# Two runs of eight: a second wait in front of the ninth indirect transfer of a row scatter and of a row gather

## The reference

```python
    h = _L0_tok_ref(x, codebook, W1, b1, W2, b2)               # take rows, gelu(q W1 + b1) W2 + b2
    h = h + _L0_attn_ref(_layernorm(h), Wz, bz, Wh, bh)        # two minGRU layers
    h = h + _L0_ffn_ref(_layernorm(h), w1s, w2s, w3s, W1, W2, W3, Wg)

    # the feed-forward stage
    shared = geglu(xf, w1s, w2s, w3s)                          # (gelu(x w1) * (x w2)) w3
    idx = jnp.argmax(xf @ Wg, axis=-1)
    for e in range(8):
        final = final + jnp.where((idx == e)[:, None], geglu(xf, W1[e], W2[e], W3[e]), 0.0)
    return shared + final
```

## Time and profile before

| | |
|---|---|
| device time, median of 3 | 533.82 us (533.76 to 534.25) |
| profiled execution, its own time | 534.71 us |
| its span | 533.1 us |
| PE busy | 503.7 us, 94% |
| DVE, ACT, POOL busy | 323.8, 247.2, 74.5 us |
| mean granted clock of PE | 0.982 of full |
| scatter: 16 transfers issued | 247.44 to 268.38 us |
| gather of results: 16 transfers issued | 493.62 to 514.55 us |

### The profile page before, as it was taken

The page is one execution under the profiler, slowest core; times in us unless marked ns, Lnnn a source line. Parts: engine busy times, 40 slices in busy tenths (PEclk is TensorE's granted clock), DMA queues, the critical chain, the costliest instruction groups (busy, mean ns, idle before and its releaser), DMA issues.

```text
span 533.1 us, 9472 instructions
## 1 busy us (share of the span) xinstructions
PE 503.7 (94%) x2942; PEld 441.1 (83%) x2943; DVE 323.8 (61%) x533; ACT 247.2 (46%) x374; POOL 74.5 (14%) x97
## 2 busy tenths in 40 slices
PE   8999998998999997999899799999999999999975
PEld 7798887886887786888788689898898988888864
DVE  2547677787587777657443847734865568383325
ACT  2656673564663453334243645724563555362311
POOL 4422030000000000003710001000100001000740
PEclk9999998999999999999999899999999999999978
DMA  5941412000020002202332338440546165200324
GB/s 169 317 164 29 144 39 80 0 1 1 2 80 1 1 0 80 79 1 81 132 114 90 123 145 271 142 148 30 183 163 205 42 253 192 105 20 20 88 71 157
DMA packets 20586, 52.81 MB, mean 99 GB/s; under 512 B 3280, under 2 KB 14544, under 8 KB 16592
## 3 DMA queue, kind: packets, MB, share of 16 engines
q0 software_dynamic: 5328, 28.32, 15.1%
q1 hardware_dynamic: 15232, 24.15, 13.7%
HBM read 41.71 MB, written 10.75 MB: 98 GB/s over the span
## 4 chain that ended last, share of the span: by engine, by line
PE 82%; DVE 10%; ACT 4%; issue 3%; POOL 0%; another core or an unknown queue 0%; DVEq 0%; ACTq 0%
PE ps L240 24%; PE ps L242 24%; PE ps L241 24%; PE ps L686 3%; PE ps L432 2%; PE ps L595 1%; DVE hs L1062 1%; DVE v_gate L1050 1%; DVE xn L1034 1%; DVE w_slots L981 1%; DVE hT L953 1%; DVE v_gate L1053 1%; PE ps L610 1%; ACT a_gate L821 1%; ACT t_gate L819 1%
## 5 line engine op out<-in xcount | busy, mean ns | idle before, releaser
L953 DVE TENSOR_TENSOR hT<-ps,hT 128x512 fp32r<-128x512 f32 x64 | 44.1, 689 | 46.4 <-ACT hT L761 25.2
L240 PE MATMUL ps<-w_slots,xTp 128*128 (+1 forms) x160 | 64.9, 406 | 1.4 <-issue 1.4
L1256 DVE TENSOR_TENSOR w_slots<-stage,w_slots 128x2048 f32 x24 | 55.0, 2292 | 13.6 <-ACT w_slots L893 11.4
L242 PE MATMUL ps<-w_slots,xTp 128*128 (+1 forms) x160 | 63.1, 394 | 0.0
L241 PE MATMUL ps<-w_slots,xTp 128*128 (+1 forms) x160 | 62.9, 393 | 0.0
L240 PE MATMUL ps<-w_slots,gTp 128*128 (+1 forms) x160 | 46.8, 293 | 0.0
L959 DVE TENSOR_TENSOR ps<-ps,gelub 128x512 f32<-128x512 f32 x32 | 22.3, 696 | 40.4 <-PE ps L242 20.2
L772 ACT ACTIVATE hT<-ps 128x512 fp32r<-128x512 f32 x32 | 19.1, 598 | 57.8 <-DVE ps L959 56.2
L242 PE MATMUL ps<-w_slots,gTp 128*128 (+1 forms) x160 | 45.3, 283 | 0.0
L241 PE MATMUL ps<-w_slots,gTp 128*128 (+1 forms) x160 | 45.2, 283 | 0.0
L759 ACT ACTIVATE ps<-ps,b 128x512 f32<-128x512 f32 x32 | 21.2, 661 | 51.1 <-PE ps L242 49.5
(11 more groups left out here) (184 smaller groups left out, 1287.4 us busy)
## 6 DMA issues: line engine op xcount, KB each, us to landing
stage<-ew_in POOLq DMA_DIRECT2D x18, 1024.0 KB, 5.1
stage<-ew_in SPq DMA_DIRECT2D x6, 1024.0 KB, 4.8
x_sorted<-zero_row SPq DMA_DIRECT2D x23, 128.0 KB, 3.8
x_row<-x_sorted SPq DMA_DIRECT2D x21, 128.0 KB, 2.1
y_sorted<-y_row SPq DMA_DIRECT2D x20, 128.0 KB, 1.7
out_rows<-fetched SPq DMA_DIRECT2D x3, 512.0 KB, 3.2
first_stage<-tok_w_in SPq DMA_DIRECT2D x1, 1024.0 KB, 5.0
first_stage<-tok_w_in SPq DMA_DIRECT2D x2, 512.0 KB, 4.6
```

Of the source, the lines that this page charges most:

```text
L240: pe.matmul(dst, lhs_hi, rhs_hi, start=start, stop=False, skip_group_check=shares_bank)
L242: return pe.matmul(dst, lhs_lo, rhs_hi, start=False, stop=stop, skip_group_check=shares_bank)
L953: dve.tensor_tensor(hT[:, c % RING, 1, :], ps[:, bank, :], f32(hT[:, c % RING, 0, :]), ALU.subtract).then_inc(h_lo, 1)
L1256: dve.tensor_tensor(w_slots[:, bass.ds(to + (PART + c * WCH), WCH)], stage[:, c, :], f32(w_slots[:, bass.ds(to + c * WCH, WCH)]), ALU.subt ...
```

## The change

In front of the ninth transfer of each of the two series, POOL gets one more wait. In the scatter it is on `h_lo` reaching `RANK + 7` = 51, that is the low part of chunk 50. In the gather it is on `h_lo` reaching `AHEAD + 4` = 60, the low part of chunk 59. Nothing else differs.

```diff
             for t in range(TILES):
+                if t == TILES // 2:
+
+                    pool.wait_ge(h_lo, RANK + 7)
                 pool.indirect_dma_start(
                     out=x_sorted, out_offset=bass.IndirectOffsetOnAxis(ap=pos[:, t:t + 1], axis=0),
                     in_=xn2[:, t, :], in_offset=None,
...
             for t in range(TILES):
+                if t == TILES // 2:
+                    pool.wait_ge(h_lo, AHEAD + 4)
                 pool.indirect_dma_start(
                     out=fetched[:, t, :], out_offset=None, in_=y_sorted,
                     in_offset=bass.IndirectOffsetOnAxis(ap=pos[:, t:t + 1], axis=0),
```

## The result

| | before | changed |
|---|---|---|
| median, us (6 runs each) | 533.92 (533.71 to 534.25) | 532.11 (530.26 to 532.87) |
| ratio of the times | | 0.9959, 95% interval 0.9942 to 0.9976 |
| profiled execution, its own time | 534.71 | 532.87 |
| span | 533.1 | 531.2 |

The forecast was 530.7, the range 529.5 to 537.5. The profiled execution is the slowest of the six of the changed kernel. The ratio is that of the means of the six, so it isn't quite the quotient of the two medians.

What follows compares the result with a forecast made beforehand. PE bounds the kernel, losing time where it stands still or runs at half clock near POOL's indirect transfers. Profiled 534.71 - 3.53 (scatter) + 0.4 (sorted rows) = 531.6, median 0.89 lower: 530.7 us, range 529.5 to 537.5.

Steps and rivals of the forecast that it cites:

- What bounds it: Whole kernel: PE, busy nearly throughout, loses time at standstills and half clock near POOL's indirect transfers, some 9 us together.
- The gather's wait is open: Gather's ninth transfer: chunk 59's low part is done 2.9 us before the wait is reached; gain 0, loss 0.
- The scatter's gain: Chunk 50 at the scatter: standstill goes, gaining 3.53 us, of which 2.07 is waiting and 1.46 half clock.
- The first sorted rows as the tight place: After the scatter: x_row lands at 278.6, PE wants it at 279.48, 0.9 us to spare; 0.4 us of waiting taken.
- No standstill in a run of eight: Split series of transfers: ACT and DVE do not stand still within eight transfers; a standstill there would mean being wrong.
- my own list: Signs of being wrong: ACT or DVE standing still in eight transfers, x_row landing after 281, a hole in the gather.
- Another cause for the standstill: Around 261 us: DVE and ACT stand still for reasons unrelated to the run's length, so chunk 50 ends at 272.69.
- slower rival: Scatter: ninth transfer opens late, PE waits 3.0 us for sorted rows plus 1.46 of clock; 538.3 us, chance 0.24.
- The total: Whole kernel: 534.71 - 3.53 + 0.4 = 531.6 us profiled; 530.7 for the median, which lies 0.89 lower.

Runs made afterwards that it cites:

- experiment 1: The changed kernel without the gather's wait, only the scatter's on chunk 50's low part: 532.98 us, 0.9917 of the kernel before.
- experiment 2: The changed kernel without the scatter's wait, only the gather's on chunk 59's low part: 536.82 us, 0.9990 of the kernel before.
- experiment 9: Kernel before with forty direct POOL transfers (24 to a spare array first) replacing the scatter's sixteen indirect ones, sort left out: 532.96 us, one execution.
- experiment 10: Kernel before with the scatter's sixteen indirect transfers moving a quarter of each row to an unread array: 535.62 us, one execution.
- experiment 3: Kernel before with only a gather's wait, moved to chunk 61's low part so that it bites: 536.03 us, 0.9954 of the kernel before.
- experiment 8: Kernel before with the scatter's sixteen transfers made direct, in token order, sort left out: 534.03 us, one execution.
- experiment 11: The changed kernel unaltered, run again on another chip: 531.61 us, 0.9910 of the kernel before.
- experiment 4: Kernel before with only a scatter's wait, one chunk later on chunk 51's low part: 538.58 us, 1.0017 of the kernel before.

## Why the prediction was right, and where not

- **What bounds it.** Right. PE's standstill at chunk 50 and the half clock behind it (0.66 of full from 265 to 270 us) were the scatter's, as experiments 1, 2, 9 and 10 show: the clock stayed at 1.00 from 255 to 280 us in 1 and 9, and was 0.66 from 270 to 275 in 2 and 0.50 from 265 to 270 in 10. The earlier trace rows has two slices at 8 tenths ahead of the end and not one: 80 to 93 us and 293 to 307 us, each at 0.87. Neither is the scatter's; they are patches of the kind described above.
- **The gather's wait is open.** Right: no hole, and alone it changes nothing (0.9990).
- **The scatter's gain.** I had 3.53 less 0.4 us, 3.1 net. The profile shows 3.86 net, from 23.54 and 19.68 us; between the up products of chunks 50 and 52 alone it is 12.42 - 8.36 = 4.06. The gain without the wait for the sorted rows was short by 0.5: I had kept the 0.40 us by which PE waited for the first `add_rows` as normal, and it went too. It was a third standstill, which the name of a releaser had hidden. DVE's product of chunk 49 stands 3.88 us behind the start of its up product (255.29) before, and 3.02 us behind it (257.39) in the changed kernel, so DVE was late by 0.86 us already at 259.17, right behind the eighth transfer. The same wait is 2.42 to 2.47 us in experiments 2, 3 and 10 and 1.52 or 1.53 us in 1, 8, 9 and 11:

```profile
259.17 0.70 DVE L959 TENSOR_TENSOR ps<-ps,gelub 128x512 f32<-128x512 f32 x1 [2.40 <-PE ps L242]
```
```profile
260.41 0.70 DVE L964 TENSOR_TENSOR ps<-ps,gelub 128x512 f32<-128x512 f32 x1 [1.53 <-issue]
```

- **The first sorted rows as the tight place.** Right as a place, by terms that offset each other. On the changed kernel's clock, which is 2.10 us behind, the low part of chunk 50 was due at 267.46; it was done at 266.64, since the standstill before it went too. From there to the ninth transfer (267.44) it took 0.80 us where I had put none, and from the last packets to SP's load some 0.5 where I had 0.1. PE lost 0.2 us: the transposes start 0.44 us behind the last matmul of the up product, where before it was 0.24. I had taken 0.4. Together with the term above, the net gain was short by 0.7 us. For experiment 4 I had expected 5.5 us and the medians gave 5.6, but not by the parts that I had named: 4.18 us of later start and 2.4 us of half clock, where I had 4 and 1 to 1.5; together 6.6 in the profile.
- **No standstill in a run of eight.** Wrong as stated, and by my own list a sign of being wrong. ACT stands still for 2.6 to 4.1 us in the scatter's second run, in every kernel with the rest. That the time was right all the same is owed to where it falls: it had cover, and PE, which sets the time, never waited for it.
- **Another cause for the standstill.** The slower rival, 538.3, rested on one and did not come. ACT did not stand still for the whole of the scatter before, but for 8.10 us from 261.02 on, 13.6 us after the first transfer. Beside 21 us of direct transfers (experiment 9) PE, ACT and DVE went on; beside sixteen indirect ones (experiments 2 and 10) DVE stood still for 2.86 and 2.87 us and ACT for 8.76 and 9.51. Whether it is the transfers that hold them or POOL's work for them, no run tells.
- **The total.** 532.11 in place of 530.7. In the profiled execution the stage from chunk 50 to the transposes gained 0.7 us more than forecast and the part ahead of it lost 2.10, most of it to half clock; the two offset in part, and that is luck. The other five executions, 530.26 the fastest, left no trace, so for the median it is likely but not shown. I had no term for the clock's spread, since the first three times of the kernel before lay within 0.5 us. In the timed runs on the chip of experiments 1 to 4 the kernel before had its slowest executions (538.9 us and more) at a mean granted clock of 0.976 to 0.979 and its fastest (533.86) at 0.989.

What stays open is the path: how a series of indirect transfers holds DVE, ACT and, at the gather, even PE between two matmuls of one group, where the program has no wait. In the kernel before PE stands still there four times, 2.98 us in all; the second row is the second matmul of a group of three:

```profile
511.59 0.39 PE L240 MATMUL ps<-xb_last,w_slots 128*128 128x512 f32 x1 [1.19 <-issue]
...
513.73 0.49 PE L241 MATMUL ps<-xb_last,w_slots 128*128 128x512 f32 x1 [1.02 <-issue]
```

Also open is why ACT is held 7 us into the second run of eight of the scatter and not in the first, nor in the gathers with a rest. All of this was read under the profiler; the medians of the timed runs moved with it.

## What to carry to other kernels

If idleness without a named releaser falls within a long series of indirect transfers, look for whether an engine on the critical path is the one held, and try a rest in the middle by a wait on the work that goes on beside it; 2.6 and 3.0 us were enough here. Look also for idleness whose named releaser had been done long before: three of the four ACT standstills at the unsplit scatter bear a name. Check in the trace that the wait is still closed when it is reached, for the open wait of experiment 2 cost nothing and did nothing: moved by one chunk, the gather's went from 0 to 4.8 us of the tail (38.95 and 34.15 us). And check who waits for the last transfer of the series: the place for the rest is bounded on the other side, where 4.18 us more cost 5.6 by the medians.

## What was not expected of the hardware

- Beside sixteen indirect transfers of 128 rows in a row DVE stood still for 2.2 to 2.9 us and ACT for 8.1 to 9.5 us at the scatter, and PE for 2.98 us in all at the gather of the kernel before, between its matmuls; beside forty direct ones of the same size from the same engine PE was busy for 21.40 of 21.40 us, and no rest of DVE or ACT was longer than 2.39 us.
- A quarter of the bytes changed neither POOL's 1.28 us for a transfer nor DVE's 2.87 us nor ACT's standstill (9.51 us).
- The granted clock of one stretch of equal work was 1.00 in one execution and 0.69 in another, behind the same wait of PE of 2.82 us; a patch like this cost 1.3 to 2.8 us.
